# One-core vision block with a mixture of experts: gate columns stored in two places of the sync queue, with half of the first expert's weights before the late ones

## The chip, the cores and the metric

The kernel is one launch on one core of a Trainium2 chip. The metric is the time of that launch on the device, in microseconds; lower is better.

## What is computed

64 images of 3x96x96 are cut into 36 patches of 768 values each. The reference then does this (all in float32):

```python
z = _layernorm(patches, ln1_g, ln1_b)
z = einsum('bnp,pe->bne', z, W_proj) + b_proj
z = _layernorm(z, ln2_g, ln2_b)
h = concatenate([cls, z], axis=1) + pos_emb            # 64 x 37 rows of 256
h = h + attention(_layernorm(h))                       # one head, the diagonal masked
xn = _layernorm(h)
topv, topi = top_k(softmax(xn @ router_w + router_b), 2); topv /= topv.sum(-1)
# each of 8 experts keeps its 444 rows of largest topv (capacity)
xin = x_flat[tok]; hid = gelu(xin @ w1[e] + b1[e])     # 256 -> 1024
out_e = (hid @ w2[e] + b2[e]) * w                      # 1024 -> 256
out = zeros.at[tok].add(out_e)
h = h + (layernorm(out) * ln_g + ln_b)
```

## The kernel before, in words

**Stage 1, the token pipeline (0 to about 178 us).** Three images make one tile of 111 live rows out of 112, so there are 22 tiles (TILES). Every engine runs the same software pipeline of 28 steps (`pipeline`, STEPS = TILES + 6): step i handles tile i in one part, tile i - 1 in the next and so on; steps below some number and those of the tail are written out, the rest is a hardware loop. At the end each tile has its row-normalised input x2 (VectorE and GpSimd make mean and root, ScalarE makes x2 in `norm_row`, L487 stores it) and its base row H. GpSimd adds the output bias `lnb` to H (L1624) and counts semaphore `hb`; SyncE then stores H twice, into the DRAM table x2_rows (L506, 224 KB as two copies) and as the first value of the output (L509, 111 KB). SyncE's part of step i stores x2 of tile i - 4 and H of tile i - 6. x2_rows has rows of 513 floats: x2, H, and in the last column the gate.

**Stage 2, the routing (about 178 to 226 us).** VectorE makes the two best experts and their gates of tiles 0 to 15 (EARLY = 16) in the tail of stage 1, at `gates(0, EARLY, 1)` in step TILES + 1, and those of tiles 16 to 21 after the pipeline; each ends with `.then_inc(r_V, 1)` at L1162. Then the kernel finds, for each expert, the 444th largest gate by a search in 8 rounds (L1290 to L1301). In a round VectorE counts one part of the gates (L1290), ScalarE the other with Sign (L710), TensorE adds up the counts (L920), VectorE makes the next candidates (L1301). ScalarE's program also holds, between the rounds r = 3, 4, 5 and 6, the conversions of the first expert's weights (`w1_high(0, 0)`, `w2_high(0, 0)`, `w1_high(0, 1)`, `w2_high(0, 1)`; L684 and L690). Each waits for the first half of w1 or w2 (`w1_in[0]`, `w2_in[0]`), and the next round's Sign stands behind it in ScalarE's order. After the search VectorE makes one-hot tables, TensorE turns them into the row list of the first expert (L932), VectorE reads it (L1339, semaphore `r_idx0`). TensorE then has `keep_clock(24)`: 48 passes of matmuls (L939) that nobody reads.

**Stage 3, the experts (from about 222 us to the end).** GpSimd gathers the listed rows of x2_rows with indirect DMAs (L1649, four of 112 rows for one expert). Before the first of these it waits for `r_idx0`, and for every store into the tables: `x2_out`, `s_fill`, `g_col` (the gate columns, 64 = four stores of 16), `h_out`, `o_pre`. TensorE transposes the first expert's rows in pairs (`first_gathered`, L953), with the lists of all experts between the pairs (`lists`, L944); the pair of matmul loops `hidden` (L977) and `project` (L994) follow, eight experts one after another. From the second expert on SyncE loads w1 and w2 in halves as their buffers come free.

**SyncE's order around the change.** All stores and weight loads named here are issued by SyncE to one queue, in the order of its program. After the pipeline's last step it waits until the input buffers, which share memory with the weights, are free (`x_n`, `xT_ps`, `z_ps`), and issues the four halves of the first expert's weights (`load_w1`, 512 KB by the page, L517; `load_w2`, L522), then the gate columns: `store_gates(0, EARLY)` once `r_V` is 1, `store_gates(EARLY, TILES)` once it is 2 (L450). A gate column is written as single floats, 2052 bytes apart in DRAM: the early call makes two DMAs of 7.0 KB (1,792 floats each), the late call two of 2.6 KB (672 floats each).

Of the kernel before, what the change touches and what calls it, by code (L numbers as in the profile page):

```python
# [44 lines left out]
def vit_tower(nc, x, ln1_g, ln1_b, w_proj, b_proj, ln2_g, ln2_b, cls_token, pos_emb,  # L45
# [6 lines left out]
    TILES = -(-IMAGES // PER)  # L52
# [3 lines left out]
    E, _, HID = w1.shape  # L56
    HC = HID // 128
# [4 lines left out]
    EARLY = 16  # L62
# [11 lines left out]
    with ctx:  # L74
# [51 lines left out]
        w1r = stage[:, 0:EC * HID].rearrange("p (c h) -> p c h", c=EC)  # L126
        w2r = stage[:, EC * HID:2 * EC * HID].rearrange("p (k o) -> p k o", k=HC)
# [181 lines left out]
        x_n = sem("x_n")  # L309
        xT_ps = sem("xT_ps"); xT_sb = sem("xT_sb"); z_ps = sem("z_ps"); xT_lo = sem("xT_lo")  # L310
# [39 lines left out]
        def live(t):  # L350
            return not isinstance(t, int) or 0 <= t < TILES
# [81 lines left out]
        @block.sync  # L433
        def _(sp):

            def load_x(t, slot):
                n = min(PER, IMAGES - PER * t) if isinstance(t, int) else PER
                for m in range(PER):
                    if m < n:
                        src = x[PER * t + m] if isinstance(t, int) else \  # L440
                            x[bass.ds(t * PER + m, 1)].rearrange("a r f -> (a r) f")
                        sp.dma_start(xin[m * L + 1:(m + 1) * L, slot, :], src).then_inc(x_in[slot], 16)

            x2_v = x2_blocks[0:P, 2:Q + 2, 0:ED]
            hb_v = x2_blocks[0:P, 2:Q + 2, ED:GC]
            gate_v = x2_blocks[0:P, 2:Q + 2, GC:XW].rearrange("p (t k) a -> p k (t a)", k=2)

            def store_gates(a, b):
                for k in range(2):
                    sp.dma_start(gate_v[:, k, a:b], gate[:, k, a:b], allow_slow_non_contiguous=True).then_inc(g_col, 16)  # L450
            for t in range(2):
                sp.wait_ge(s_xz, t + 1)
                load_x(t, t)

            def load(done, dst_, src):
                sp.dma_start(dst_, src).then_inc(done, 16)  # L456

            sp.wait_ge(s_zero, 1)
            for m in range(PER):
                load(c_g, g2m[m * L + 1:(m + 1) * L, :], rep(ln2_g, 0, PATCHES))  # L460
                load(c_g, posadd[m * L + 1:(m + 1) * L, :], rep(ln2_b, 0, PATCHES))
                load(c_g, posadd[m * L:m * L + 1, :], cls_token)
                load(c_g, posb[m * L:(m + 1) * L, :], pos_emb)
            load(c_a, wq[:, :, :], wq_t.rearrange("(c p) o -> p c o", p=128))
            load(c_a, wk[:, :, :], wk_t.rearrange("(c p) o -> p c o", p=128))
            load(c_a, wv[:, :, 0:ED], wv_t.rearrange("(c p) o -> p c o", p=128))
            load(c_a, bqk[:, 0:EC], bq)
            load(c_a, bqk[:, EC:2 * EC], bk)
            load(c_a, bvb[:, 0:ED], rep(bv, 0, P))
            load(c_a, rw[:, :, :], router_w.rearrange("(c p) e -> p c e", p=128))  # L470
            load(c_a, rbb[:, :], rep(router_b, 0, P))

            for t in range(2, 4):
                sp.wait_ge(s_xz, t + 1)
                load_x(t, t)

            def step(i, slot):
                par = slot % 2
                t = i + 4
                if live(t):  # L480
                    need(sp, x_n, i + 1)
                    load_x(t, slot)
                t = i - 4
                if live(t):
                    need(sp, x2_ok, t + 1)
                    dram = x2_v[:, 2 * t:2 * t + 2, :] if isinstance(t, int) else x2_v[:, bass.ds(t * 2, 2), :]
                    sp.dma_start(dram, rep(x2[:, slot:slot + 1, :], 1, 2)).then_inc(x2_out[slot], 16)  # L487
                if isinstance(i, int) and i == 1:
                    load(c_l, lng[:, :], rep(ln_g, 0, P))
                    load(c_l, lnb[:, :], rep(ln_b, 0, P))  # L490
                    load(c_l, b1t[:, :], b1)
                    sp.dma_start(b2t[:, :], b2.rearrange("a (k p) -> p (a k)", p=128),
                                 allow_slow_non_contiguous=True).then_inc(c_l, 16)
                if isinstance(i, int) and i == 18:
                    sp.wait_ge(s_xz, 5)
                    sp.dma_start(x2_blocks[0:P, 0:2, :], rep(zero[:, :].rearrange("p (a f) -> p a f", a=1), 1, 2))\
                        .then_inc(s_fill, 16)
                    sp.dma_start(sums[0:1, :], zero[0:1, 0:ED]).then_inc(s_fill, 16)
                    sp.dma_start(x2_blocks[P:128, :, :],
                                 rep(zero[0:128 - P, 0:XW].rearrange("p (a f) -> p a f", a=1), 1, Q + 2)).then_inc(s_fill, 16)  # L500
                t = i - 6
                if live(t):
                    need(sp, hb, t + 1)
                    tile = H[:, t:t + 1, 0:ED] if isinstance(t, int) else H[:, bass.ds(t, 1), 0:ED]
                    dram = hb_v[:, 2 * t:2 * t + 2, :] if isinstance(t, int) else hb_v[:, bass.ds(t * 2, 2), :]
                    sp.dma_start(dram, rep(tile, 1, 2)).then_inc(h_out, 16)  # L506
                    n = LIVE_LAST if isinstance(t, int) and t == TILES - 1 else PER * L
                    dram = out[PER * L * t:PER * L * t + n, :] if isinstance(t, int) else out[bass.ds(t * (PER * L), n), :]
                    sp.dma_start(dram, tile[0:n, :, :].rearrange("p a f -> p (a f)")).then_inc(o_pre, 16)  # L509
            pipeline(sp, step, 9, 17)  # L510


            HALF_H, HALF_K = HID // 2, HC // 2

            def load_w1(e, h):
                cols = slice(h * HALF_H, (h + 1) * HALF_H)
                sp.dma_start(w1r[:, :, cols], w1[e].rearrange("(c p) h -> p c h", p=128)[:, :, cols])\  # L517
                    .then_inc(w1_in[h], 16)

            def load_w2(e, h):  # L520
                ks = slice(h * HALF_K, (h + 1) * HALF_K)
                sp.dma_start(w2r[:, ks, :], w2[e].rearrange("(k p) o -> p k o", p=128)[:, ks, :])\  # L522
                    .then_inc(w2_in[h], 16)

            sp.wait_ge(x_n, TILES)
            sp.wait_ge(xT_ps, TILES)
            sp.wait_ge(z_ps, TILES)
            for h in range(2):
                load_w1(0, h)
                load_w2(0, h)  # L530
            for a, b, n in ((0, EARLY, 1), (EARLY, TILES, 2)):
                sp.wait_ge(r_V, n)
                store_gates(a, b)
            sums_v = sums[1:1 + E * SLOTS, :].rearrange("(c p) f -> p c f", p=P)

            def store_sums(e):
                sp.wait_ge(y_sb, (e + 1) * JT)
                sp.dma_start(sums_v[:, e * JT:(e + 1) * JT, :], sm[:, :, :]).then_inc(s_out, 16)

            sp.wait_ge(g_in[0][JT - 1], 16)  # L540
            for e in range(1, E):
                for h in range(2):
                    if h and e > 1:
                        store_sums(e - 2)
                    sp.wait_ge(w1_lo, 4 * (e - 1) + 2 * h + 2)
                    load_w1(e, h)
                    sp.wait_ge(w2_lo, 4 * (e - 1) + 2 * h + 2)
                    load_w2(e, h)
            store_sums(E - 2)


            sp.wait_ge(o_out, 16 * JT * E)
            sp.wait_ge(o_pre, 16 * TILES)
            sp.wait_ge(h_out, 16 * TILES)
            sp.wait_ge(s_out, 16 * (E - 1))
            sp.wait_ge(s_fill, 48)
            sp.wait_ge(g_col, 64)
            for k in range(4):
                sp.wait_ge(x2_out[k], 16 * ((TILES - k + 3) // 4))
# [954 lines left out]
        def _(pool):  # L1514
# [77 lines left out]
            def step(i, slot):  # L1592
                par = slot % 2
                on = [k for k, back in enumerate((0, 1, 4)) if live(i - back)]
                if on:
# [16 lines left out]
                    for k, done in ((1, h_nb), (2, g_nb)):  # L1612
                        if k == 1 and k in on:
                            G.tensor_tensor(dev[:, par:par + 1], norm(par, 0, 1), norm(par, 1, 1), ALU.mult).then_inc(h_dev, 1)
                        if k in on:
                            k = 1 if last else k
                            G.tensor_scalar(norm(par, 2, k), nmv[:, k, 0:1], norm(par, 1, k), -1.0, ALU.mult, ALU.mult)\  # L1617
                                .then_inc(done, 1)
                for t in range(i - 6, i - 4) if isinstance(i, int) and i == TILES + 3 else (i - 5,):
                    if live(t) and not (isinstance(i, int) and i == TILES + 2):  # L1620
                        if isinstance(t, int) and t == 0:
                            pool.wait_ge(c_l, N_L)
                        need(pool, x2_ok, t + 1)
                        G.tensor_tensor(tile_of(H, t), tile_of(H, t), lnb[:, :], ALU.add).then_inc(hb, 1)  # L1624
# [108 lines left out]
```

## Time and profile before

| | |
|---|---|
| median of 3 runs | 414.99 us (413.75 to 417.43) |
| the profiled execution | 417.57 us, its span 415.7 us |
| TensorE busy in the span | 348.5 us (84%) |
| VectorE busy | 319.1 us (77%) |
| ScalarE busy | 254.7 us (61%) |
| GpSimd busy | 222.5 us (54%) |
| mean granted TensorE clock | 0.917 of full |
| DMA in the span | 57.29 MB in 49,278 packets, 12,248 of them under 512 bytes |

The span runs from the first to the last instruction of the profiled execution, and all positions below are microseconds from its start. PE is TensorE's matmuls, DVE VectorE, ACT ScalarE, POOL GpSimd; SPq is SyncE, whose only work is to issue DMAs. In a timeline a row gives start, duration, engine, line, operation and shapes, and in brackets how long the engine had been idle and what ended that. In the chain of work that ended last a row gives start, duration and what the chain went through: an instruction, a DMA in flight, or "issue".

### The profile page before, as it was taken

What the parts mean: (1) busy time and instruction counts of PE and PEld (TensorE: products, weight loads), DVE (VectorE), ACT (ScalarE), POOL (GpSimd) and SP (SyncE); (2) the same over time, 40 slices, a digit from 0 to 9 for tenths busy, and PEclk for the clock granted to TensorE, in tenths of its full rate; (3) what the DMA queues carried; (4) which work ended last, traced back from release to release, by engine and by line L of the source; (5) the groups of instructions that cost most, each with busy time, mean ns of one, the idle gap of its engine ahead of it and who ended that gap; (6) DMA issues with size and microseconds to landing.
All of it is one profiled execution on the core that took longest, in us unless ns stands there. A gap on an engine that the chain in (4) does not pass through costs nothing.

```text
span 415.7 us, 7904 instructions
## 1 busy us (share of the span) xinstructions
PE 348.5 (84%) x2128; PEld 307.8 (74%) x2128; DVE 319.1 (77%) x874; ACT 254.7 (61%) x552; POOL 222.5 (54%) x377
## 2 busy tenths in 40 slices
PE   2799999999999998540038999999999999999960
PEld 0588888887888886230028899999999999999950
DVE  7674778878888877879887655878787878787954
ACT  3255587767868775644700378686868686868620
POOL 4154776666666764430004443057777777645675
PEclk9898999999999999955557699999999999999996
DMA  6641024545454389678812386655858595852221
GB/s 174 188 88 37 30 58 129 147 128 139 126 151 135 95 134 118 163 196 248 39 0 68 115 254 187 184 147 149 231 165 249 151 243 168 244 171 76 62 83 45
DMA packets 49278, 57.29 MB, mean 138 GB/s; under 512 B 12248, under 2 KB 38229, under 8 KB 49244
## 3 DMA queue, kind: packets, MB, share of 16 engines
q1 hardware_dynamic: 42602, 43.11, 40.0%
q0 software_dynamic: 5568, 13.00, 12.0%
q10 hardware_dynamic: 1074, 0.79, 0.7%
q8 instruction: 14, 0.23, 0.2%
q14 instruction: 20, 0.16, 0.2%
HBM read 36.74 MB, written 21.36 MB: 140 GB/s over the span
## 4 chain that ended last, share of the span: by engine, by line
PE 56%; issue 10%; SPq 8%; POOL 8%; DMA 7%; DVE 6%; ACT 3%; ACTq 0%; DVEq 0%; POOLq 0%
PE pz L977 18%; PE pall L994 17%; PE pall L837 5%; DMA x_rows<-gate 5%; PE pall L805 3%; PE pall L812 3%; SPq L456 2%; SPq L450 2%; POOL nrm L1609 2%; PE pall L1005 1%; DMA stage<-in_x 1%; PE pall L963 1%; SPq L509 1%; PE pall L821 1%; PE pz L785 1%
## 5 line engine op out<-in xcount | busy, mean ns | idle before, releaser
L994 PE MATMUL pall<-halves 128*128 128x444 f32 x384 | 88.5, 365 | 0.8 <-DVE halves L1398 0.8
L977 PE MATMUL pz<-halves 128*128 128x444 f32 x384 | 89.1, 368 | 0.0
L977 PEld LDWEIGHTS pz<-halves 128*128 128x128 f32 x384 | 73.6, 192 | 5.0
L994 PEld LDWEIGHTS pall<-halves 128*128 128x128 f32 x384 | 70.8, 188 | 6.0 <-DVE halves L1398 1.1
L1649 POOL DMA_INDIRECT held<-x_rows,gidx x32 | 35.8, 1119 | 64.3 <-issue 50.4
L738 ACT ACTIVATE wproj<-pz,b1t 128x444 f32<-128x444 f32 x64 | 40.5, 633 | 45.3 <-PE pz L977 44.7
L1398 DVE TENSOR_TENSOR halves<-wproj,halves 128x444 fp32r<-128x444 f32 x64 | 39.8, 622 | 28.2 <-ACT halves L750 22.1
L837 PE MATMUL pall<-halves 128*112 128x256 f32 x396 | 56.6, 299 | 3.2 <-DVE halves L1089 3.2
L837 PEld LDWEIGHTS pall<-halves 128*112 128x112 f32 x396 | 51.3, 183 | 5.1 <-DVE zbias L1108 2.4
L1673 POOL DMA_INDIRECT out<-rows,didx x28 | 37.0, 1323 | 22.7 <-DVE rows L1446 15.4
L750 ACT CAST halves<-wproj 128x444 fp32r<-128x444 f32 x64 | 36.1, 564 | 2.0
L1657 POOL DMA_INDIRECT rows<-sums,sidx x28 | 29.7, 1060 | 7.8 <-issue 7.5
L633 ACT ACTIVATE x<-held,nrm 112x256 f32 (+1 forms) x22 | 13.2, 602 | 25.6 <-POOL nrm L1617 15.2
L1368 DVE TENSOR_TENSOR halves<-stage,halves 128x512 fp32r<-128x512 f32 x32 | 22.0, 687 | 7.0 <-ACT halves L684 7.0
L805 PE MATMUL pall<-x1T,wq 128*128 128x112 f32 x176 | 24.9, 285 | 1.9 <-ACT x1T L677 0.7
L576 ACT ACTIVATE stage<-stage,rs 112x768 f32<-112x768 f32 x22 | 22.4, 1019 | 4.6 <-POOL rs L1554 4.6
L805 PEld LDWEIGHTS pall<-x1T,wq 128*128 128x128 f32 x176 | 21.3, 191 | 5.2 <-ACT x1T L677 3.6
L1080 DVE BATCH_NORM_STATS2 xstat<-stage 112x6 f32<-112x384 f32 x44 | 22.3, 549 | 3.2 <-DMA stage<-in_x 3.2
L812 PE MATMUL pall<-wv,x1T 128*112 128x273 f32 x88 | 23.9, 394 | 0.0
L1630 POOL TENSOR_TENSOR held<-held,posb 112x256 f32 (+1 forms) x22 | 16.2, 738 | 11.4 <-ACT held L638 10.2
L1609 POOL TENSOR_TENSOR nrm<-nrm,neghalf 112x3 f32<-112x3 f32 (+2 forms) x26 | 21.1, 811 | 2.3 <-POOL nrm L1607 0.2
L1374 DVE TENSOR_TENSOR halves<-stage,halves 128x512 fp32r<-128x512 f32 x32 | 22.0, 688 | 0.0
(283 smaller groups left out, 716.4 us busy)
## 6 DMA issues: line engine op xcount, KB each, us to landing
stage<-in_w SPq DMA_DIRECT2D x32, 512.0 KB
stage<-in_x SPq DMA_DIRECT2D x64, 108.0 KB
x_rows<-x SPq DMA_DIRECT2D x22, 224.0 KB, 3.1
x_rows<-held SPq DMA_DIRECT2D x22, 224.0 KB, 4.2
sums<-rows SPq DMA_DIRECT2D x7, 448.0 KB
out<-held SPq DMA_DIRECT2D x21, 111.0 KB
x_rows<-zero SPq DMA_DIRECT2D x1, 1474.9 KB
wproj<-in_w_proj ACTq DMA_DIRECT2D x1, 768.0 KB
```

Source lines behind the costliest of these rows:

```text
L738: nc.scalar.activation(hr[:, k % 2, 0:CAP], bank(k % 2)[:, 0:CAP], ACT.Gelu, bias=col(b1t, u)).then_inc(u_sb, 1)
L750: nc.scalar.copy(hh[:, k % 2, 0:CAP], hr[:, k % 2, 0:CAP]).then_inc(h_hi, 1)
L805: m = nc.tensor.matmul(bank(3)[:, o * P:(o + 1) * P], wqk[:, c, o * 128:(o + 1) * 128], xt_[:, c, :], start=(c == 0), stop=(c == EC - 1))
L812: m = nc.tensor.matmul(bank(4)[0:P, 0:VW], xt_[:, c, :], wv[:, c, :], start=(c == 0), stop=(c == EC - 1))
L837: nc.tensor.matmul(bank(2)[0:P, 0:ED], xs[:, c * P:(c + 1) * P], w[:, c, :], start=(c == k == 0), stop=False)
L977: m = nc.tensor.matmul(bank(k % 2)[:, 0:CAP], w[:, c, k * 128:(k + 1) * 128], xs[:, e % 2, c, 0:CAP], start=(n == 0), stop=(n == 3 * EC - 1))
L994: m = nc.tensor.matmul(pall[:, 2 * (e % 2) + o, 0:CAP], w[:, k, o * 128:(o + 1) * 128], hs[:, k % 2, 0:CAP], start=(k == 0 and n == 0), st ...
L1398: V_.tensor_tensor(hl[:, k % 2, 0:CAP], hr[:, k % 2, 0:CAP], hh[:, k % 2, 0:CAP].bitcast(fp32), ALU.subtract)\
L1609: G.tensor_tensor(nrm[:, par, 1, a:b], nrm[:, par, 0, a:b], rep(neghalf[:, :], 1, b - a), ALU.pow)\
L1649: pool.indirect_dma_start(xg[:, e % XB_N, j, :], None, x2_rows, bass.IndirectOffsetOnAxis(ap=gidx[:, k:k + 1], axis=0)).then_inc(g_in[e % ...
L1657: pool.indirect_dma_start(prev[:, j, :], None, sums[0:1 + e * SLOTS, :], bass.IndirectOffsetOnAxis(ap=sidx[:, k:k + 1], axis=0)).then_inc( ...
L1673: pool.indirect_dma_start(out, bass.IndirectOffsetOnAxis(ap=didx[0:n, k:k + 1], axis=0), final_of(e)[0:n, j, :], None, bounds_check=IMAGES ...
```

## The change

Three edits.

1. SyncE's pipeline, step TILES + 3 (25): waits for `r_V` 1 and stores the early gates, ahead of that step's x2 store of tile 21 and H stores of tile 19.
2. SyncE's pipeline, step TILES + 4 (26): waits for the input buffers and loads the first halves of w1 and w2, ahead of the H stores of tile 20. After the pipeline it waits for `r_V` 2, stores the late gates, and then loads the second halves of w1 and w2. The two load functions are the same, only defined earlier.
3. GpSimd's pipeline: the bias adds to H. Before, tile 18 is done in step 23, none in step 24, tiles 19 and 20 in step 25, tile 21 in step 26. Now tiles 18 and 19 are done in step 23, none in steps 24 and 25, and tiles 20 and 21 in step 26 behind a wait for `r_V` 2.

```diff
             def step(i, slot):
                 par = slot % 2
+                if isinstance(i, int) and i == TILES + 3:
+                    sp.wait_ge(r_V, 1)
+                    store_gates(0, EARLY)
+                if isinstance(i, int) and i == TILES + 4:
+                    sp.wait_ge(x_n, TILES)
+                    sp.wait_ge(xT_ps, TILES)
+                    sp.wait_ge(z_ps, TILES)
+                    load_w1(0, 0)
+                    load_w2(0, 0)
                 t = i + 4
                 if live(t):
                     need(sp, x_n, i + 1)
...
             pipeline(sp, step, 9, 17)
...
-            sp.wait_ge(x_n, TILES)
-            sp.wait_ge(xT_ps, TILES)
-            sp.wait_ge(z_ps, TILES)
-            for h in range(2):
-                load_w1(0, h)
-                load_w2(0, h)
-            for a, b, n in ((0, EARLY, 1), (EARLY, TILES, 2)):
-                sp.wait_ge(r_V, n)
-                store_gates(a, b)
+            sp.wait_ge(r_V, 2)
+            store_gates(EARLY, TILES)
+            load_w1(0, 1)
+            load_w2(0, 1)
...
-                for t in range(i - 6, i - 4) if isinstance(i, int) and i == TILES + 3 else (i - 5,):
-                    if live(t) and not (isinstance(i, int) and i == TILES + 2):
+                if isinstance(i, int) and i == TILES + 4:
+                    pool.wait_ge(r_V, 2)
+                for t in {TILES + 1: (i - 5, i - 4), TILES + 2: (), TILES + 3: (), TILES + 4: (i - 6, i - 5)}.get(i, (i - 5,)) \
+                        if isinstance(i, int) else (i - 5,):
+                    if live(t):
                         if isinstance(t, int) and t == 0:
                             pool.wait_ge(c_l, N_L)
                         need(pool, x2_ok, t + 1)
```

## Rows read from the trace of the kernel before

**Rows 1.** The page's 40 slices of about 10.4 us: TensorE busy, and its clock.
```profile
PE   2799999999999998540038999999999999999960
PEclk9898999999999999955557699999999999999996
```

**Rows 2.** The chain of work that ended last, 193 to 234 us.
```profile
193.32 1.93 SPq L450
195.29 5.76 SPq L450
...
201.42 0.61 SPq L450
...
202.09 18.98 DMA x_rows<-gate
...
221.31 0.96 issue
222.27 1.84 POOL held L1649
...
227.06 3.33 DMA held<-x_rows,gidx
...
231.08 2.01 PE pall L944 x22
```

**Rows 3.** Timeline of DVE: a search round, its wait for ACT, the first list's reading.
```profile
197.22 1.85 DVE L1290 TENSOR_SCALAR_CACHE_REDUCE wproj<-scratch,cand 128x1568 bf16<-128x1568 f32 x1
...
199.72 0.22 DVE L1293 TENSOR_SCALAR won<-cnt,signs 128x1 bf16<-128x1 f32 x1 [0.65 <-ACT junka L710]
...
218.75 0.15 DVE L1339 TENSOR_SCALAR gidx<-pall 112x4 uint32<-112x4 uint32 x1
```

**Rows 4.** Timeline of ACT: end of round 3's count, then the first weight conversion.
```profile
195.74 0.19 ACT L710 ACTIVATION_READ_ACCUMULATOR junka<-keysa,canda 128x1 f32 x1
197.73 0.62 ACT L684 CAST halves<-stage 128x512 fp32r<-128x512 f32 x1 [1.80 <-DMA stage<-in_w]
```

**Rows 5.** Timeline of DVE and POOL around the routing of the last tiles.
```profile
178.33 2.10 POOL L1624 TENSOR_TENSOR held<-held,lnb 112x256 f32<-112x256 f32 x3
...
178.39 0.74 DVE L1132 TENSOR_TENSOR LG<-LG,rbb 112x48 f32<-112x48 f32 x1 [1.52 <-ACT LG L654]
...
179.43 0.38 DVE L1135 TENSOR_TENSOR eqm<-LG,m 112x48 f32<-112x48 f32 x1
179.84 0.65 DVE L1136 TENSOR_TENSOR eqm<-eqm,erev 112x48 f32<-112x48 f32 x1
...
181.79 0.21 DVE L1136 TENSOR_TENSOR eqm<-eqm,erev 112x48 f32<-112x48 f32 x1
...
185.24 0.21 DVE L1162 TENSOR_TENSOR V<-V 112x48 f32<-112x48 f32 x1
...
185.55 0.62 DVE L1276 TENSOR_SCALAR keysa<-scratch 128x896 int32<-128x896 int32 x1
```

**Rows 6.** Timeline of the sync queue's DMA issues in the tail.
```profile
182.70 0.82 SPq L487 DMA_DIRECT2D x_rows<-x  x1
...
186.11 0.51 SPq L506 DMA_DIRECT2D x_rows<-held  x1
...
190.07 0.40 SPq L517 DMA_DIRECT2D stage<-in_w  x1
```

**Rows 7.** The instructions on the tile gate: its stores, and their time to landing.
```profile
L450 SPq DMA_DIRECT2D x_rows<-gate x4: 612/3176/5756, 193.3 to 202.1; - x4
...
DMA to landing us min/median/max: 13.8/15.4/19.0
```

**Rows 8.** Timeline of PE between the search and the first expert.
```profile
218.31 8.06 PE L939 MATMUL pall<-ident 128*128 128x128 f32 x48
226.56 0.42 PE L953 MATMUL pall<-ident,held 112*128 112x112 f32 x2 [0.18 <-DMA held<-x_rows,gidx]
227.84 0.41 PE L953 MATMUL pall<-ident,held 112*128 112x112 f32 x2 [0.86 <-DMA held<-x_rows,gidx]
228.08 1.31 PE L944 MATMUL pall<-ohvals,rows 112*112 112x64 bf16 x22
...
230.44 0.64 PE L953 MATMUL pz<-ident,held 112*128 112x112 f32 x2 [0.80 <-DMA held<-x_rows,gidx]
```

More of the change, by code:

```diff
@@ L475, in _, with load_w1, load_w2 @@
                 load_x(t, t)
+            HALF_H, HALF_K = HID // 2, HC // 2
+            def load_w1(e, h):
+                cols = slice(h * HALF_H, (h + 1) * HALF_H)
+                sp.dma_start(w1r[:, :, cols], w1[e].rearrange("(c p) h -> p c h", p=128)[:, :, cols])\
+                    .then_inc(w1_in[h], 16)
+            def load_w2(e, h):
+                ks = slice(h * HALF_K, (h + 1) * HALF_K)
+                sp.dma_start(w2r[:, ks, :], w2[e].rearrange("(k p) o -> p k o", p=128)[:, ks, :])\
+                    .then_inc(w2_in[h], 16)
             def step(i, slot):
                 par = slot % 2
+                if isinstance(i, int) and i == TILES + 3:
[7 more added lines that the diff above has]
+                    load_w2(0, 0)
                 t = i + 4
@@ L510, in _ @@
             pipeline(sp, step, 9, 17)
[L513 to L523, printed above, removed]
-            sp.wait_ge(x_n, TILES)
-            sp.wait_ge(xT_ps, TILES)
-            sp.wait_ge(z_ps, TILES)
-            for h in range(2):
-                load_w1(0, h)
-                load_w2(0, h)
-            for a, b, n in ((0, EARLY, 1), (EARLY, TILES, 2)):
-                sp.wait_ge(r_V, n)
-                store_gates(a, b)
+            sp.wait_ge(r_V, 2)
+            store_gates(EARLY, TILES)
+            load_w1(0, 1)
+            load_w2(0, 1)
             sums_v = sums[1:1 + E * SLOTS, :].rearrange("(c p) f -> p c f", p=P)
```

## The prediction

> **What bounds the kernel now.** I read the page's slices first. TensorE is busy nearly everywhere except in slices 16 to 22 (about 156 to 229 us), and its granted clock is at half (1.2 GHz of 2.4) in most of that stretch [rows 1]. The change touches only this gap, so what it can win or lose lies between two marks: the end of the token pipeline, near 178 us, and the first expert's matmuls, near 233 us. Next I read the chain of waits [rows 2]. Through the gap it does not run over the search. It runs over the sync queue: two early gate stores issued at 193.32 and 195.29, two late ones at 201.42 and 202.09, then 18.98 us of a gate store in flight until 221.07, then GpSimd's first gather at 222.27, whose fourth part lands at 227.06 + 3.33 = 230.39, and TensorE's lists at 231.08. So the gather waits for the gate column. The timeline of VectorE gives the other condition of the gather: the first list is read at 218.75 + 0.15 = 218.90 [rows 3]. The gates are therefore only 221.07 - 218.90 = 2.17 us later than the list. That is all that the gate's wait costs; what remains is the chain of the search.
>
> I then asked what the search itself waits for. Round 4's count on VectorE was over and VectorE sat idle 0.65 us until ScalarE's count came [rows 3]. ScalarE had finished round 3 at 195.93 and was idle 1.80 us, until a weight load let `w1_high(0, 0)` start at 197.73 [rows 4]. So the landing of the first half of w1 already sets the search by 0.65 us, and the change puts two gate stores in front of that load.
>
> **Part 1, the late gates go ahead of half the weights, the early ones far ahead.** Late stores: they no longer wait behind the early ones' 1.93 + 5.76 us of issue [rows 2]; those go to 182.70, where the x2 store of tile 21 was [rows 6]. I bound the landing of the last gate. From the latest issue that I can make, SyncE has all that it had before except two weight halves, so it issues the last gate no later than 202.09; the same 18.98 us would end at 221.07, no gain. The shortest flight of the four is 13.8 us [rows 7], and an issue near 200 gives 214. The flights are long because gate stores queue behind each other: two are in flight when the late ones are issued, and here the early ones are 10 us further ahead. I take 214. It is 5 us before the list is read, so the gate leaves the chain and the list at 218.90 takes its place.
>
> **Part 2, the bias adds.** Three adds ran at 178.33 for 2.10 us, 0.70 us each. VectorE's routing of the last tiles ran under them: L1132 took 0.74, L1135 0.38 and L1136 0.65 us, where an operation of the same shape without GpSimd at work takes 0.21 (L1136 at 181.79) [rows 5]. That is 0.53 + 0.17 + 0.44 = 1.14 us on VectorE's chain into the search, which goes. The two adds behind `r_V` 2 come at about 185.45 + 0.1, at the same time as L1276 (0.62 us, begins at 185.55) [rows 5]. If the add begins first it holds up L1276 by up to 0.7 us; if it comes second, nothing. The add of tile 19, moved to step 23, falls near 172.8 beside the early gates' small operations: from nothing to 0.7 us. I take 0.2 for both together, 1.4 as the bad end. Search start: 0.9 us earlier (from 0.3 later to 1.1 earlier). H of tiles 20 and 21 is ready at about 187.1, while SyncE reaches its store after the weights, past 190, so that wait costs nothing.
>
> **Part 3, the first half of w1.** Now 182.70 to 190.07 holds x2 of tile 21 and H of tiles 19, 20 and 21 [rows 6]. After the change H of 20 and 21 goes behind the weights: from 186.11 to 190.07 [rows 6], 3.96 us of queue come out from before the load. The two early gate stores come in. Lower bound: each costs what the first did, 1.93 us, so 3.86 in all (this first one was not held up); and below that nothing, if other stores are still in front anyway. Upper bound: 1.93 + 5.76 = 7.69 [rows 2]. I take 5.0, nearer to the lower end, since the 5.76 was spent with four weight halves (2 MB) waiting in front, and at 182.70 there is only about half a megabyte. The load is then issued 1.0 us later and lands at 197.73 + 1.0 = 198.8 (bounds: 193.8 with the gates free, 201.5).
>
> What does the search do with that? Call c the shift of everything from round 4 on. The load decides as soon as it comes after the point at which ScalarE wants it: c = (landing - 197.73), but not below -(0.65 + 0.9) = -1.6. With 198.8, c = +1.05; with 193.8, -1.6; with 201.5, +3.8. So the 0.9 us of part 2 is swallowed by this wait: the search begins earlier and stands at round 4.
>
> **The sum.** The list is read at 218.90 + c. GpSimd needs about 1.3 us from the release to the first gather (221.07 to 222.27, and one more wait) [rows 2], so it starts at 220.2 + c, 2.1 - c earlier than now; the fourth part lands at 228.3 + c. But TensorE has its 8.06 us of `keep_clock` in front, which begin with the list (218.31) and end at 226.37 [rows 8]; now the gather comes 0.2 us after that end. After the change TensorE is the late one: 226.4 + c, two pairs of transposes (0.4 each), 22 list matmuls (1.3), two pairs more (0.4 each), ending at 229.4 + c, the DMA's own end being 228.3 + 0.6 + c. Today this point is 230.44 + 0.64 = 231.08 [rows 8]. The difference is 1.7 - c. With c = 1.05 that is a gain of 0.65 us; at the best end 3.3 us, at the late end (3.8) a loss of 2.1 us. From there on the experts' stage is the same and the clock rises with the same work before it, so I carry the difference to the end. The profiled execution of 417.57 us would become 416.9. It stands 2.6 us above the median, and I apply the difference to the median: 414.99 - 0.65 = 414.3 us. A measurement of this kernel tells about 1% (4.2 us) from no change.
>
> **The rivals.**
> - *The weights arrive in time (chance 0.27).* Gate packets are tiny, and if they slip through in little time the load lands before 196. For it: the price of a gate store ahead of a load stands in no row, and the 1.93 us that the first one took to issue may hide behind the stores in front of it. Against it: the second took 5.76 us [rows 2]. The list is read at 217.3, the gain is 3.3 us, 411.7 us. The list and `keep_clock`, not the gates, then bound the gap, so no more can come out.
> - *The weights' landing waits for the gate stores' landings (0.25).* A gate store takes 13.8 to 19.0 us from issue to landing [rows 7]. If nothing behind it on the queue counts as landed earlier, the w1 half is not there until the second early store is: issued at 182.70 + 1.93 = 184.6, flying 15.5 us (the median [rows 7]), 200.1, or 203.6 at the longest flight of 19.0. Then c is 2.4 to 5.9, and the loss 0.7 to 4.2 us; centre 2.4, 417.4 us. It decides from a landing of 199.4 on, where c passes 1.7. Against it: the weights were always ahead of the gates, so no row shows the order reversed.
>  The Trainium skill (DMA: Bandwidth & Descriptors, section "Queues, rings and completion order") states such a rule: a DMA's semaphore increment is a strongly ordered write, which lands only after every earlier write from that DMA engine. No row here shows it for a load behind a gate store; by it this rival would be the forecast.
> - *The gates stay late (0.05).* If the late stores still fly 19 us from an issue after 200, the gather waits until 219 to 221 as now, and nothing moves: 415.0.
> - The forecast, c near 1: 0.43.
>
> **How the numbers follow.** Above 1% faster needs over 4.2 us; only the first rival with something unseen reaches it: 0.06. Above 1% slower needs c near 5.9, the long end of the second rival, or a disturbance in the experts' stage: 0.10. Within 1%: 0.84. The range takes both rivals in: from 411.7 less 0.9 for the spread of a median to 417.4 plus 0.7: 410.8 to 418.1.
>
> **What would show it right or wrong.** Right: the last gate lands before 216; GpSimd's first gather is released by the list's reading; the ScalarE idle before the first L684 is above 3 us, ended by the load; L1132 takes 0.2 us; the first L953 follows L939 with no gap. Wrong in part 3: L684 starts straight behind the count of round 3, or VectorE's idle in round 4 exceeds 4 us. Wrong in the sum: another engine's wait in the 233 us region grows by what was gained.

## The result, and the profile after

The changed kernel takes 419.92 us (median of 6 runs, 419.29 to 422.18), the kernel before 414.37 us on the same chip: a ratio of 1.0152, 95% interval 1.0113 to 1.0191. It is 5.5 us slower; the forecast was 0.65 us faster, with a range up to 418.1. Every ratio here compares only executions within 1.5% of the fastest of their kernel, which among others leaves out two of the six of the kernel before (417.43 and 1890.57 us) and six of the ten of x7 below.

In the profiled execution (419.37 us, span 417.3) the chain of work that ended last no longer passes a gate store in flight, but a weight load:

```profile
189.22 0.68 SPq L530
...
190.02 13.42 DMA stage<-in_w
...
204.22 1.14 ACT junka L714 x2
...
224.65 0.30 issue
224.95 1.82 POOL held L1656
...
230.05 3.63 DMA held<-x_rows,gidx
...
233.73 0.42 PE pz L957 x2
```

The half of w1 was issued at 190.02, at the same point of the span as before (190.07, [rows 6]), and flew (time from its issue to its landing) 13.42 us instead of some 7.7. ScalarE and VectorE show who waited. First ScalarE, then VectorE (start, duration, operation, idle before):

```profile
193.31 0.19 ACT L714 ACTIVATION_READ_ACCUMULATOR junka<-keysa,canda 128x1 f32 x1
203.46 0.62 ACT L688 CAST halves<-stage 128x512 fp32r<-128x512 f32 x1 [9.97 <-DMA stage<-in_w]
```

```profile
196.55 0.08 DVE L1294 DVE_READ_ACCUMULATOR wproj<-scratch,cand 128x1 f32 x1
205.45 0.22 DVE L1297 TENSOR_SCALAR won<-cnt,signs 128x1 bf16<-128x1 f32 x1 [8.81 <-ACT junka L714]
...
224.49 0.15 DVE L1343 TENSOR_SCALAR gidx<-pall 112x4 uint32<-112x4 uint32 x1
```

These answer to [rows 4] and [rows 3]: ScalarE's idle before its first conversion grew from 1.80 to 9.97 us, VectorE's in round 4 from 0.65 to 8.81, and the first list is read at 224.64 instead of 218.90. The sync queue in the same stretch:

```profile
179.76 5.96 SPq L450 DMA_DIRECT2D x_rows<-gate  x2
185.77 2.90 SPq L508 DMA_DIRECT2D x_rows<-x  x1
188.71 0.47 SPq L527 DMA_DIRECT2D x_rows<-held  x1
189.22 0.68 SPq L530 DMA_DIRECT2D out<-held  x1
190.02 0.40 SPq L481 DMA_DIRECT2D stage<-in_w  x1
```

The two early stores together took 5.96 us to issue and landed at 191.12 and 200.64; the x2 store behind them, issued at 185.77, landed at 201.51, and the H store at 201.26. So the two stores issued next behind the gates landed together just after the second gate store, and w1 2.8 us behind it. The engines' transfers show that this is no matter of a semaphore alone. Windows of the changed kernel (busy times of PE, PEld, DVE, ACT, POOL, then clock, DMA share, GB/s; the share sums the times of single packets, and as these overlap it can pass 1):

```profile
186.00:188.00 2.00, 0.16 (x1) 0.10 (x1) 1.82 (x7) 1.00 (x2) 0.00 (x0) 0.50 0.81 4
188.00:190.00 2.00, 0.19 (x1) 0.11 (x1) 1.89 (x7) 0.75 (x4) 0.00 (x0) 0.50 0.81 53
190.00:192.00 2.00, 0.19 (x1) 0.10 (x1) 1.93 (x6) 0.92 (x2) 0.00 (x0) 0.50 1.46 47
192.00:194.00 2.00, 0.00 (x0) 0.00 (x0) 1.95 (x3) 1.33 (x3) 0.00 (x0) 0.50 1.00 59
```

and of the kernel before, profiled once more (next section):

```profile
186.00:188.00 2.00, 0.76 (x5) 0.41 (x3) 1.92 (x6) 1.62 (x4) 0.00 (x0) 0.50 0.42 134
188.00:190.00 2.00, 0.16 (x1) 0.10 (x1) 1.83 (x7) 0.17 (x3) 0.00 (x0) 0.50 0.53 162
190.00:192.00 2.00, 0.00 (x0) 0.00 (x0) 1.96 (x3) 1.31 (x3) 0.00 (x0) 0.50 0.84 272
192.00:194.00 2.00, 0.18 (x1) 0.10 (x1) 1.93 (x5) 1.33 (x3) 0.00 (x0) 0.50 1.00 272
```

With the gates in front the DMA engines count as busy (0.81 to 1.46) and move 4 to 59 GB/s; without them they move 134 to 272. The packets of the stretch from 190 to 194 us, first in the changed kernel, then in x0:

```profile
DMA packets 252, 0.21 MB, mean 53 GB/s; under 512 B 69, under 2 KB 229, under 8 KB 252
...
q1 hardware_dynamic: 252, 0.21, 123.4%
```

```profile
DMA packets 845, 1.09 MB, mean 272 GB/s; under 512 B 30, under 2 KB 597, under 8 KB 845
...
q1 hardware_dynamic: 845, 1.09, 92.1%
```

From the shares (16 engines, 4 us) a packet took 0.31 us on average in the changed kernel and 0.07 us in x0. The half of w1 is 256 packets of 2 KB, and in the changed kernel no other load or store of the stretch has packets of that size: 23 of them moved from 190 to 194, 131 from 194 to 200 and 102 from 200 to 204. So w1's data itself came late, and not only the signal of its landing. The gate stores' own packets were over much earlier: 3,633 packets under 512 B moved from 181 to 191 us and 56 from 191 to 201, while the second of these stores counted as landed at 200.64.

### The profile page after: what moved, and what is told of

It is laid out like the page before. It is cut to its first block, busy times and chain, and to the rows that moved or that the text cites. A ratio compares the mean times of both kernels' runs of the same rounds, so it can differ in the third digit from the quotient of the medians.

```text
span 417.3 us, 7905 instructions
## 1 busy us (share of the span) xinstructions
PE 345.2 (83%) x2128; PEld 304.3 (73%) x2128; DVE 318.6 (76%) x874; ACT 254.3 (61%) x552; POOL 225.7 (54%) x377
## 4 chain that ended last, share of the span: by engine, by line
PE 56%; DVE 12%; issue 11%; POOL 8%; ACT 4%; DMA 4%; SPq 3%; ACTq 1%; DVEq 0%; POOLq 0%
PE pall L998 17%; PE pz L981 17%; PE pall L841 5%; DMA stage<-in_w 3%; PE pall L809 3%; PE pall L816 2%; POOL nrm L1613 2%; PE pall L1009 1%; SPq L450 1%; PE pall L967 1%; PE pall L781 1%; PE pz L789 1%; PE pall L825 1%; POOL held L1656 1%; POOL held L1637 1%
## 5 line engine op out<-in xcount | busy, mean ns | idle before, releaser
L981 PE MATMUL pz<-halves 128*128 128x444 f32 x384 | 87.1, 362 | 0.1
L981 PEld LDWEIGHTS pz<-halves 128*128 128x128 f32 x384 | 71.9, 188 | 5.0 <-DVE halves L1413 0.2
L1656 POOL DMA_INDIRECT held<-x_rows,gidx x32 | 37.4, 1169 | 59.8 <-DVE gidx L1343 39.9
L841 PE MATMUL pall<-halves 128*112 128x256 f32 x396 | 55.4, 295 | 2.2 <-DVE halves L1093 2.2
L841 PEld LDWEIGHTS pall<-halves 128*112 128x112 f32 x396 | 50.2, 180 | 4.0 <-DVE zbias L1112 2.4
L1680 POOL DMA_INDIRECT out<-rows,didx x28 | 37.0, 1323 | 21.6 <-DVE rows L1450 15.1
L637 ACT ACTIVATE x<-held,nrm 112x256 f32 (+1 forms) x22 | 13.2, 602 | 25.8 <-POOL nrm L1621 15.5
L1372 DVE TENSOR_TENSOR halves<-stage,halves 128x512 fp32r<-128x512 f32 x32 | 22.0, 686 | 7.1 <-ACT halves L688 6.0
L924 PE MATMUL pz<-won,grp 128*128 128x1 bf16 x8 | 1.5, 184 | 29.5 <-DVE won L1297 26.2
L688 ACT CAST halves<-stage 128x512 fp32r<-128x512 f32 x32 | 19.7, 616 | 10.0 <-DMA stage<-in_w 10.0
L816 PE MATMUL pall<-wv,x1T 128*112 128x273 f32 x88 | 24.8, 406 | 0.0
```

The costliest lines, as they stand in the source:

```text
L816: m = nc.tensor.matmul(bank(4)[0:P, 0:VW], xt_[:, c, :], wv[:, c, :], start=(c == 0), stop=(c == EC - 1))
L841: nc.tensor.matmul(bank(2)[0:P, 0:ED], xs[:, c * P:(c + 1) * P], w[:, c, :], start=(c == k == 0), stop=False)
L981: m = nc.tensor.matmul(bank(k % 2)[:, 0:CAP], w[:, c, k * 128:(k + 1) * 128], xs[:, e % 2, c, 0:CAP], start=(n == 0), stop=(n == 3 * EC - 1))
L1656: pool.indirect_dma_start(xg[:, e % XB_N, j, :], None, x2_rows, bass.IndirectOffsetOnAxis(ap=gidx[:, k:k + 1], axis=0)).then_inc(g_in[e % ...
L1680: pool.indirect_dma_start(out, bass.IndirectOffsetOnAxis(ap=didx[0:n, k:k + 1], axis=0), final_of(e)[0:n, j, :], None, bounds_check=IMAGES ...
```

## The experiments

The theory after the result (A): a load behind the early gate stores lands late because these drain slowly, and ScalarE's conversion, which stands between two rounds, turns that into a stop of the search. The rivals: the split of the weight halves or the bias adds cost the time (B); the tail's backlog of 111-row output stores costs it (F). Whether another queue would save it is D against E. C asks whether the first profiled execution of the kernel before was a usual one.

All kernels in one table, from their profiles: start of the first conversion, which is the landing of w1 where ScalarE was waiting for it (marked *); VectorE's idle in round 4; the first list read; the last gate's landing; start of the first `project` matmul (L994 of the kernel before); and the ratio to the kernel before, run on the same chip, with its 95% interval. The chips differ between the experiments (the kernel before had medians of 413.1, 413.4 and 416.8 us on three of them), so times of different experiments are compared by their ratios.

| kernel | first conversion | round 4 idle | list read | last gate | `project` | ratio |
|---|---|---|---|---|---|---|
| before, first profile | 197.73* | 0.65 | 218.90 | 221.07 | 237.53 | |
| before, again (x0) | 196.41 | 0.04 | 218.86 | 217.20 | 233.39 | |
| changed | 203.46* | 8.81 | 224.64 | 213.11 | 239.21 | 1.0152 (1.0113 to 1.0191) |
| x1 bias adds only | 195.61 | 0.04 | 218.06 | 215.93 | 232.62 | 1.0003 (0.9968 to 1.0039) |
| x2 early gates only | 206.11* | 9.91 | 227.27 | 211.55 | 241.85 | 1.0324 (1.0276 to 1.0372) |
| x3 weights first | 195.84 | 0.04 | 218.29 | 213.16 | 233.23 | 1.0021 (0.9984 to 1.0058) |
| x4 conversions last | 205.29* | 0.04 | 216.14 | 215.14 | 230.76 | 0.9997 (0.9962 to 1.0032) |
| x5 gates behind | 193.51 | 0.04 | 215.96 | 214.06 | 230.57 | 0.9955 (0.9914 to 0.9996) |
| x7 gates on another queue | 202.90* | 6.53 | 234.16 | 215.43 | 249.07 | 1.0074 (1.0007 to 1.0142) |
| x8 rows spread | 203.27* | 6.71 | 224.44 | 213.22 | 239.12 | 1.0128 (1.0054 to 1.0202) |
| x10 one early store | 198.63* | 1.91 | 219.83 | 217.10 | 234.45 | 0.9994 (0.9957 to 1.0031) |
| x11 x5 again | 196.06 | 0.04 | 218.52 | 219.40 | 234.97 | 0.9980 (0.9941 to 1.0019) |

In all rows the time from the first `project` matmul to the span's end is 178.1 to 178.5 us: whatever happens before it is carried to the end unchanged. Stage 1 itself differs by 2.7 us from execution to execution: VectorE's first operation on the last tiles (L1132 of the kernel before) starts at 177.09 in the changed kernel and at 179.75 in x11. Where that matters I count from this operation: w1 lands 26.4 us behind it in the changed kernel, and 19.3 in the first profile of the kernel before.

**x0, the kernel before once more.**

> The kernel before, profiled once more. Theory C (the first profiled execution, 417.57 us, had gate stores that landed unusually late): the last gate lands before the list is read, the gather is released by the list, and the time is 411 to 414 us. Rival (the gates are what the gather waits for in every execution): gather released by a gate landing 2 us or more after the list, about 415 to 417 us.

It took 413.68 us. The list, and not a gate, released the gather:

```profile
219.17 1.82 POOL L1649 DMA_INDIRECT held<-x_rows,gidx  x1 [38.16 <-DVE gidx L1339]
```

and ScalarE found the weights there (conversion at 196.41, straight behind the count that started at 196.31). Theory C holds as far as one more execution can show it: of the two waits that I had read in the first profile, the gather's for the gate and round 4's for w1, this one has neither. Both executions read the list at the same time (218.90 and 218.86), but `project` starts 4.1 us later in the first. The gather began 3.1 us later there (222.27, [rows 2]), and the last transposes ended 2.75 us later. The other 1.4 us are TensorE's clock. The kernel before, first profile, then x0, from the end of the transposes on:

```profile
231.00:237.00 6.00, 6.00 (x34) 5.62 (x33) 3.98 (x14) 1.99 (x4) 2.81 (x3) 0.50 0.19 45
```

```profile
229.00:234.00 5.00, 3.76 (x24) 3.16 (x23) 4.71 (x15) 2.81 (x6) 3.17 (x2) 1.00 0.26 61
```

After `keep_clock` both stood at the full clock. In the first profile TensorE was then busy for 2.20 of the 3 us from 228 to 231, waiting for gathered rows in between, and its clock fell back to half until about 237; the twelve `hidden` matmuls there took 4.59 us instead of 2.68. In x11, where the gate also came last, the clock was at half again from 231 to 234. Why it fell there and not in x1, where TensorE waited 0.95 us for the rows, is not shown.

**x2, the early gates alone.**

```diff
                 par = slot % 2
+                if isinstance(i, int) and i == TILES + 3:
+                    sp.wait_ge(r_V, 1)
+                    store_gates(0, EARLY)
...
-            for a, b, n in ((0, EARLY, 1), (EARLY, TILES, 2)):
-                sp.wait_ge(r_V, n)
-                store_gates(a, b)
+            sp.wait_ge(r_V, 2)
+            store_gates(EARLY, TILES)
```

> Edit: only the two early gate stores move to step TILES + 3; all four weight halves stay together ahead of the late gates, the bias adds stay. Theory A (loads behind the early gate stores land late and hold up the search): the first half of w1 lands at 201 to 204 us, VectorE waits 5 to 9 us in round 4, and the time is 4 to 6 us above the kernel before (418.5 to 420.5). Theory B (the loss comes from the halves being split round the late gates, or from the bias adds' wait): within 1 us of the kernel before.

The median was 424.94 us, worse than the 418.5 to 420.5 expected; its profile, at 421.86, is of the fastest of its four executions. With all H stores still in front of the weights these land at 206.11, 28.6 us behind VectorE's first operation (177.51), 2.2 us later than in the changed kernel. So this one move is the whole loss and more, and taking half of the weights ahead of two H stores wins some of it back; theory B falls. Here w1 was issued only at 195.58, 18.1 us behind the first operation against 12.9 in the changed kernel, and flew 10.5 us: the gates delay the queue's later issues as well as the flight. The second early gate store had landed at 197.03, 9.1 us before w1, so w1 did not land late merely by waiting for that store's landing.

**x3, the weights ahead of the early gates.**

```diff
                 if isinstance(i, int) and i == TILES + 3:
-                    sp.wait_ge(r_V, 1)
-                    store_gates(0, EARLY)
-                if isinstance(i, int) and i == TILES + 4:
                     sp.wait_ge(x_n, TILES)
                     sp.wait_ge(xT_ps, TILES)
                     sp.wait_ge(z_ps, TILES)
                     load_w1(0, 0)
                     load_w2(0, 0)
+                    sp.wait_ge(r_V, 1)
+                    store_gates(0, EARLY)
```

> Edit to the changed kernel: in step TILES + 3 the first halves of w1 and w2 are issued ahead of the early gate stores, everything else as changed. Theory A: the half of w1 lands before 193, VectorE's wait in round 4 is gone, the first list is read 7 to 9 us earlier than in the changed kernel, and the time is 411 to 413 us. Theory B: still 418 to 420.

413.19 us. Moving the two loads one step up, ahead of the gates (and with that of an x2 store and one tile's H stores), takes the whole loss away: w1 landed at 191.33, the wait in round 4 is gone and the list is read 6.35 us earlier, less than the 7 to 9 expected, because this execution's stage 1 was 2.4 us later (first operation at 179.54). It is no faster than the kernel before.

**x4, the conversions behind the search.**

```diff
                 signs_of(r)
-                if r >= 3:
-                    (w2_high if r % 2 == 0 else w1_high)(0, (r - 3) // 2)
+            for r in range(3, NR - 1):
+                (w2_high if r % 2 == 0 else w1_high)(0, (r - 3) // 2)
```

> Edit to the changed kernel: ScalarE's four conversions of the first expert's weights stand behind its last Sign instead of between the rounds; the queue's order stays. Theory A: the weights still land at about 203, nobody in the search waits for them, the list is read 8 us earlier than in the changed kernel; 411 to 413 us. Theory B, or if the late landing itself binds TensorE's first matmuls: 417 to 420.

411.84 us. Here the weights land as late as in the changed kernel (205.29, 27.9 us behind the first operation; ScalarE had waited 3.56 us for them after its last Sign) and it costs nothing. This separates the two halves of theory A: late weights do no harm by themselves, only the wait between two rounds does.

**x1, the bias adds alone.**

> Edit: only GpSimd's bias adds are moved, SyncE as in the kernel before. Theory A: L1132 falls from 0.74 to 0.21 us and the search begins 1 us earlier, but waits for the half of w1 and for the gates as before, so the time is 0 to 1 us below the kernel before. Theory B: H of tiles 20 and 21 waits for the late gates and holds the queue, 3 us or more above.

412.81 us, a ratio of 1.0003. The operation of the second line of [rows 5] fell from 0.74 us as expected:

```profile
179.28 0.21 DVE L1132 TENSOR_TENSOR LG<-LG,rbb 112x48 f32<-112x48 f32 x1 [1.51 <-ACT LG L654]
```

From that operation to round 0 VectorE needs 7.23 us instead of 8.37, the 1.14 us of the forecast. The expected wait for w1 did not come, as in x0. A gain of the whole time is not told apart from none.

**x5 and x11, all gate stores behind the H stores.**

```diff
-                if isinstance(i, int) and i == TILES + 3:
-                    sp.wait_ge(r_V, 1)
-                    store_gates(0, EARLY)
...
+            sp.wait_ge(r_V, 1)
+            store_gates(0, EARLY)
             sp.wait_ge(r_V, 2)
             store_gates(EARLY, TILES)
```

> Edit to the changed kernel: the early gate stores go back to just ahead of the late ones, behind all H stores; half of the weights stays ahead. Theory A: w1 lands before 195, no wait in the search; the last gate lands at 208 to 217, the list is read first; 411 to 413.5 us. Rival (splitting the weights is what costs): 417 or more.

> The same kernel as x5 (bias adds moved, half of the weights ahead, all gate stores behind the H stores), in more rounds. If its gain is the 1.1 us of VectorE that the bias adds gave back: a ratio of 0.996 to 0.999 against the kernel before, the list releasing the gather. Rival (the gain in x5 was chance): a ratio of 1.000 or above.

412.12 us (0.9955, 0.9914 to 0.9996), and in twelve executions on another chip 415.32 us against 416.83 (0.9980, 0.9941 to 1.0019). It has the other two edits and none of the loss. It is the best version tried; if it beats the kernel before, then by less than the second measurement resolves. In x11's profile the last gate landed at 219.40, after the list (218.52), and GpSimd began at 220.60, against the expectation that the list would release it: the gate's wait comes back in some executions.

**x10, one early store in front instead of two.**

```diff
-            def store_gates(a, b):
-                for k in range(2):
+            def store_gates(a, b, ks=(0, 1)):
+                for k in ks:
...
                     sp.wait_ge(r_V, 1)
-                    store_gates(0, EARLY)
+                    store_gates(0, EARLY, (0,))
...
+            store_gates(0, EARLY, (1,))
             sp.wait_ge(r_V, 2)
```

> Edit to the changed kernel: only one of the two early gate stores stays in step TILES + 3, the other goes behind all H stores, ahead of the late gates. Theory A, draining by the number of 4-byte writes: with half of them in front, w1 lands about half way between 193.5 (none in front) and 203.5 (both), at 197 to 200 us, and VectorE waits 0.5 to 3.5 us in round 4; 412.5 to 416 us. Rival (a fixed price of any gate store in front, whatever its size): w1 lands at 202 or later, 418 us or more.

w1 landed at 198.63 and VectorE waited 1.91 us, both within the expected 197 to 200 and 0.5 to 3.5. The ratio is 0.9994; the median of 416.11 us is a little above the expected 416, on a chip where the kernel before takes 416.83. Counted from VectorE's first operation, w1 is there at the latest after 16.3 us with no gate store in front (x5), after 19.5 with one and 26.4 with two. In x5 that is only a bound, as ScalarE did not wait; the trace's semaphore events put the landing at 191.32, 14.1 us behind the first operation (12.6 in x11). So each store adds its part, the first some 5 to 7 us and the second 6.9, and there is no fixed price of having one in front. Of the second's 6.9 us half is a later issue (9.5 to 12.9 us behind the first operation) and half a longer flight (10.0 to 13.4).

**x8, the output rows spread.** Each full output store of 111 rows as two, of 96 and 15.

```diff
-                    sp.dma_start(dram, tile[0:n, :, :].rearrange("p a f -> p (a f)")).then_inc(o_pre, 16)
+                    for a, b in ((0, n),) if n < 96 else ((0, 96), (96, n)):
+                        sp.dma_start(dram[a:b, :], tile[a:b, :, :].rearrange("p a f -> p (a f)")).then_inc(o_pre, 16)
...
```

> Edit to the changed kernel: each 111-row output store is issued as two, of 96 and of 15 rows. Theory F (the tail's backlog of 111-row stores, which few DMA engines carry, makes the w1 half late): the flights of the x2 stores near 175 us fall from 6 to 7 us to below 4, w1 lands before 198, the time falls below 415 us. Theory A (the gate stores' own slow draining): x2 flights may fall, but w1 still lands at 200 or later and the time stays within 1.5 us of the changed kernel (418 to 421).

The queue's backlog went: the x2 store in front of the gates flew 3.3 us instead of 7.2, the two early gate stores took 1.44 us to issue instead of 5.96, and w1 was issued at 186.68. From VectorE's first operation (179.00) that is 7.7 us, against 12.9 in the changed kernel, so 5.2 us earlier. The landing came only 2.1 us earlier (24.3 us behind it, against 26.4), after a flight of 16.6 us:

```profile
203.27 0.62 ACT L689 CAST halves<-stage 128x512 fp32r<-128x512 f32 x1 [7.87 <-DMA stage<-in_w]
```

The time was 419.68 us, a ratio of 1.0128 (1.0054 to 1.0202, four executions), not told apart from the changed kernel's. Theory F explains at most those 2.1 us of an idle that is still 6.71; most of the earlier issue was lost again in flight. In the four kernels with both early gates in front, x8, the changed one, x4 and x2, w1 is issued 7.7, 12.9, 15.1 and 18.1 us behind the first operation and there after 24.3, 26.4, 27.9 and 28.6: over ten microseconds of issue move the landing by four.

**x7, the gates on GpSimd's queue.** SyncE issues no gate store; GpSimd issues all four behind its pipeline:

```diff
...
             pipeline(pool, step, 7, 19)
...
+            for a, b in ((0, EARLY), (EARLY, TILES)):
+                for k in range(2):
+                    pool.dma_start(gate_v[:, k, a:b], gate[:, k, a:b], allow_slow_non_contiguous=True).then_inc(g_col, 16)
```

> Edit to the changed kernel: GpSimd issues all four gate stores on its own queue behind its bias adds (about 185 us), SyncE's queue holds only x2, H and weights. Theory D (a load waits only behind gate stores of its own queue): w1, issued near 184 to 187, lands by 195 and the time is 411 to 413.5 us. Theory E (the DMA engines are shared, the gate packets stall them for every queue): w1 lands at 199 or later, VectorE waits in round 4, 416 us or more.

```profile
202.90 0.62 ACT L683 CAST halves<-stage 128x512 fp32r<-128x512 f32 x1 [7.68 <-DMA stage<-in_w]
```

GpSimd issued the stores from 186.67 to 190.64; w1, on the other queue since 187.10, landed at 202.90, after a flight of 15.8 us, and w2 not before 215.63, so that VectorE waited 10.12 us more in round 5. Another queue was no way round in this execution, as theory E says. The ten times scatter from 414.87 to 429.70 us, with a median of 421.93, and the profiled execution is the slowest of them, so its numbers stand for how bad it can be; where w1 landed in the faster ones is not shown. No execution came into the 411 to 413.5 us of theory D, and the ratio, 1.0074 (1.0007 to 1.0142), shows no gain from the other queue.

## Why the prediction was wrong

- **What bounds the kernel: true of one execution.** The gather waited for the gate column in the profile that I read, and w1's landing held up the search by 0.65 us. In x0 neither is so. I noted that the profiled execution stood 2.6 us above the median and carried its differences over to the median unchanged. But between it and x0 the whole difference lies behind the list: 2.75 us until the last transposes and 1.4 us of clock. So the gate's wait cost that execution about 4.1 us and not the 2.17 that I gave it, and the gain term (the gate leaving the chain) most likely does not exist for the median, while the loss term does. The numbers agree: profile to profile `project` starts only 1.7 us later (237.53 to 239.21), against x0 it is 5.8 us, and the medians differ by 5.5. That this holds for most executions rests on two profiles and the medians.
- **Part 1** was right in its number, ahead of the list, but by luck: last gate foreseen at 214, landed at 213.11. It was issued at 203.66, later than the 202.09 that I called the latest possible, and flew 9.45 us, less than the 13.8 that I took.
- **Part 2** was right in size: 1.13 us of VectorE's routing went (8.37 to 7.24 us, first operation to round 0). The add of tile 19 cost 0.67 us before that stretch: under the two adds at 171.12, L1154 and L1156 ran 0.51 and 0.49 us instead of 0.16 and 0.17, inside the bound of 0.7 and more than the 0.2 taken. The two late adds held nothing up: L1280 beside them took 0.62 us as before. As foreseen, round 4's wait swallowed the rest.
- **Part 3 is the step that failed.** "The load is then issued 1.0 us later and lands at 197.73 + 1.0 = 198.8 (bounds: 193.8 with the gates free, 201.5)". I priced the gate stores by the time they take to issue and kept the flight of the load as it was. The issue was right within about a microsecond (190.02 against 191.1; counted from VectorE's first operation 1.3 us later than before, against 1.0 foreseen); the flight went from 7.7 to 13.4 us, and the landing of 203.46 lies outside my bounds. The rows had the sign of it: gate stores fly 13.8 to 19.0 us [rows 7] for a few kilobytes, so they occupied something long after the queue had let go of them. x8 shows it: issued 5.2 us earlier, the load landed 2.1 us earlier. And of the signs that I had named for an error in part 3, VectorE's idle of more than 4 us in round 4 is the one that came. All five signs that I had named for being right came too (last gate before 216, the list releasing the gather, ScalarE's idle above 3 us, L1132's operation at 0.21 us, no gap behind `keep_clock`), so none of them tested this step.
- **A rival was nearer.** "The weights' landing waits for the gate stores' landings" gave 200.1, or 203.6 at the longest flight. The second early store flew 19.6 us and w1 landed 2.8 us behind it. It had the chance 0.25, and its centre was laid on the median flight, though in the profile before the later store of each pair flew longer (15.5 and 19.0 us against 13.8 and 15.3). On a 1% slower outcome I had put 0.10. Its order of landings was seen in the changed kernel, but it is not the whole mechanism: w1's packets themselves moved late, and in x2 w1 landed 9.1 us behind the second store.
 The rule of the Trainium skill (DMA: Bandwidth & Descriptors, "Queues, rings and completion order"), that an increment lands only after the earlier writes of that DMA engine, across its queues, is not contradicted by the order of landings: w1 landed after the second early store in the changed kernel (203.46, 200.64), and in x7, where the queues differ (202.90, 201.26). It is not the whole cause, since the transfers themselves slowed down to 4 to 59 GB/s.
- **The search and the sum.** That a late load shifts the list by as much was right: w1 was there 5.73 us later (203.46 against 197.73) and the list was read 5.74 us later. From the list to the transposes the sum held roughly: I expected the last ones 4.0 us later than 231.08, and they ended at 234.14, 3.1 later, as `keep_clock` took 7.39 us instead of 8.06. From the list to the first gather I gave 1.3 us; released by the list it took 0.31 (224.64 to 224.95). "From there on the experts' stage is the same and the clock rises with the same work before it" did not hold: the first profile had lost 1.4 us there to the half clock and the changed kernel did not, so `project` came only 1.7 us later. With the c that was measured, the sum would have given 414.99 + 4.0 = 419.0 for the median, near the 419.92 measured; that would have been luck, as the same sum would have missed the profiles' difference of 1.8 us.

The step that failed is thus the landing of the first half of w1, which I put 1.0 us later with its flight unchanged, where the landing came 5.7 us later. What remains open is what the 4-byte writes occupy (the DRAM side, or the DMA engines' outstanding writes) and so make other packets slow; no run separates these.

## What to carry to other kernels

In these runs a store of scattered single floats took 0.4 to 7.4 us to issue and 6 to 26 us to land, and a load behind it paid for the draining, on the same queue and, in the one execution profiled, on another: put what somebody waits for ahead of it, and price it by its flight, not by its issue. A conversion that waits for a DMA does not belong between two steps of a serial loop on another engine's critical chain, where one late landing stops everything; behind the loop it cost nothing (x4). And before a wait is removed, ask whether it is in the usual execution: where the profiled one stands above the median, the wait may be what sets it apart.

## What was not expected of the hardware

- Two DMAs of 1,792 single floats each, 7 KB, lengthened the flight of a 512 KB load issued behind them from 7.7 to 13.4 us on the same queue; with the gate stores on another queue it was 15.8 in the execution profiled. The load's own 2 KB packets moved late.
- With the gates of x7 on the second queue ten executions spread over 15 us (414.87 to 429.70); six of the changed kernel, with the same stores on the sync queue, lay within 3 us (419.29 to 422.18).
- Moving early only those gate stores cost 3.2% (x2), twice what the changed kernel loses.
- After waits for gathered rows TensorE's clock fell back to half for some 6 us in the first profile of the kernel before and for some 3 us in x11, which cost 1.4 us from the last transposes to `project` in the first.
